# Last stage of a vision tower kernel: paired decay banks, one scan over two groups, sums with h on TensorE and ScalarE, three of 24 C products on VectorE

## What is computed

```python
t = _unfold3(t, 2).transpose(0, 2, 1)
h = t @ proj_w.T + proj_b
# layer 0: h = h + ssm(layernorm(h)); h = h + ffn(layernorm(h))
A_bar = jnp.exp(dA)                                   # dA = delta * A
B_bar = (A_bar - A) / dA * delta[..., None] * Bproj[:, :, None, :]
def step(h, inp):
    a, b, c, xl = inp
    h = a * h + b * xl[..., None]
    y = jnp.einsum('bn,bdn->bd', c, h)
    return (h, y)
# ffn: a router picks one of 8 experts of 64 columns for each token (argmax), gelu, times its probability
```

## Time and profile before

| | |
|---|---|
| median of 3 runs | 9341.66 us (9338.44 to 9353.73) |
| profiled execution, device time | 9346.65 us |
| its span, first to last instruction | 9344.9 us |
| mean granted TensorE clock | 0.890 of full speed |
| last stage | from about 3640 us to the end |
| busy, share of the span | PE 82%, DVE 67%, ACT 45%, POOL 68% |

### The profile page before, as it was taken

How to read it: one execution, slowest core, us unless ns; L and a number is a source line. 1 busy time by engine, 2 the same in 40 slices (tenths; PEclk the granted TensorE clock), 3 DMA queues, 4 the chain that set the end, 5 groups by cost and what they waited for, 6 DMA issues and landing times.

```text
span 9344.9 us, 86112 instructions
## 1 busy us (share of the span) xinstructions
PE 7616.6 (82%) x30892; PEld 3189.1 (34%) x30892; DVE 6306.6 (67%) x8010; ACT 4247.4 (45%) x6801; POOL 6400.6 (68%) x2483
## 2 busy tenths in 40 slices
PE   6799999777999985578788778788778788777777
PEld 3444444223444432223333323333323333323333
DVE  1355555441233344888888888888888888888885
ACT  1366666553344432444444444444444444444442
POOL 0011111116766614999999999999999999999995
PEclk9999999998999987788888888888888888888887
DMA  0011111115444413223322323322323322323321
GB/s 25 25 39 43 44 42 38 31 31 105 96 102 97 101 37 99 84 95 115 108 97 91 118 90 119 108 97 89 118 90 118 110 97 89 116 93 112 110 97 51
DMA packets 356851, 786.54 MB, mean 84 GB/s; under 512 B 70437, under 2 KB 282806, under 8 KB 348936
## 3 DMA queue, kind: packets, MB, share of 16 engines
q1 hardware_dynamic: 320376, 690.75, 24.6%
q0 software_dynamic: 21712, 51.75, 2.2%
q10 hardware_dynamic: 14336, 38.54, 1.2%
HBM read 597.36 MB, written 183.35 MB: 84 GB/s over the span
## 4 chain that ended last, share of the span: by engine, by line
PE 25%; DVE 16%; POOL 9%; issue 8%; ACT 4%; DMA 0%; SPq 0%; DVEq 0%; POOLq 0%
PE ps L1492 7%; DVE v L1793 7%; DVE v L1802 7%; PE ps L1499 5%; PE ps L1497 5%; POOL v L1460 5%; POOL v L1450 4%; PE ps L1535 2%; PE ps L1488 2%; PE ps L1595 2%; DVE dl L1784 1%; ACT ps L1691 1%; ACT gm L1716 1%; ACT dl L1668 0%; DVE gm L1870 0%
## 5 line engine op out<-in xcount | busy, mean ns | idle before, releaser
L1691 ACT ACTIVATE ps<-dr,aa 128x448 f32<-128x448 f32 x2688 | 1695.8, 635 | 2649.4 <-DVE v L1802 2631.3
L1450 POOL TENSOR_TENSOR v<-xr,bt 128x1792 f32<-128x1792 f32 x672 | 2683.0, 3993 | 203.2 <-PE ps L1535 105.5
L1460 POOL TENSOR_TENSOR v<-v,ct 128x1792 f32<-128x1792 f32 x672 | 2690.2, 4003 | 177.7 <-ACT st L1681 177.1
L1802 DVE TENSOR_TENSOR_SCAN v<-ps,st,v 128x448 f32<-128x448 f32 x2304 | 2629.1, 1141 | 0.0
L1793 DVE SCALAR_TENSOR_TENSOR v<-ps,aa,v 128x448 f32<-128x448 f32 x2688 | 1786.6, 665 | 660.5 <-POOL v L1450 357.5
L222 POOL DMA_DIRECT2D tokens<-ob x448 | 235.4, 532 | 1883.4 <-ACT ob L383 1833.3
L1595 PE MATMUL ps<-w_or_w,gm 128*112 128x384 f32 x1792 | 737.2, 562 | 453.6 <-DVE gm L1870 382.2
L1535 PE MATMUL ps<-v,dg 128*32 128x448 f32 x5376 | 719.6, 610 | 218.5 <-POOL v L1460 217.9
L1595 PEld LDWEIGHTS ps<-w_or_w,gm 128*112 128x112 f32 x1792 | 340.5, 200 | 867.9 <-DVE gm L1870 424.6
L1492 PE MATMUL ps<-h,w_or_w 128*128 128x448 f32 x1344 | 538.4, 551 | 14.1 <-DVE gm L1837 14.1
L1488 PE MATMUL ps<-sq,jm 128*128 128x448 f32 x672 | 344.7, 658 | 191.2 <-ACT ot L1725 183.3
(11 more groups left out here) (318 smaller groups left out, 11777.1 us busy)
## 6 DMA issues: line engine op xcount, KB each, us to landing
xr<-h_by_channel SPq DMA_DIRECT2D x168, 896.0 KB, 4.7
dr<-delta_by_channel SPq DMA_DIRECT2D x168, 896.0 KB, 5.6
x<-tokens SPq DMA_DIRECT2D x252, 224.0 KB, 5.2
tokens<-ob POOLq DMA_DIRECT2D x448, 112.0 KB, 2.4
w_or_w<-in_w SPq DMA_DIRECT2D x29, 1536.0 KB, 6.3
w_or_w<-centred_w SPq DMA_DIRECT2D x27, 1536.0 KB, 6.4
h_by_channel<-h SPq DMA_DIRECT2D x112, 336.0 KB, 10.8
delta_by_channel<-dl SPq DMA_DIRECT2D x112, 336.0 KB, 5.1
```

Source lines behind the costliest of these rows:

```text
L1450: tt(v[:, n % RING], xr[:, dc % 2], bt[:, q:q + 1, :].to_broadcast([128, 4, T]), ALU.mult).then_inc(s_v, 1)
L1460: tt(v[:, n % RING], v[:, n % RING], ct[:, q:q + 1, :].to_broadcast([128, 4, T]), ALU.mult).then_inc(s_cm, 1)
L1691: fn(bank((4 * n + g) % 3), dr[:, dc % 2, g, :], ACT.Exp, scale=aa[:, 4 * k + g:4 * k + g + 1]).then_inc(s_a, 1)
L1802: nc.vector.tensor_tensor_scan(v[:, n % RING, g, :], bank((4 * n + g) % 3), v[:, n % RING, g, :], 0.0 if first else st[:, 4 * k + g:4 * k ...
```

## The change

Only `tail` changes.

- **Decays in two pairs of banks.** PSUM banks 0 to 3 hold the decays of a step's four groups: groups 0 and 1 side by side in banks 0 and 1 (the second starts at column 450 and crosses into the next bank), groups 2 and 3 in banks 2 and 3. The column ahead of each group is zero and stays so. A pair is written anew when the scan of that pair of the step before is done.
- **One scan over two groups.** v gets 449 columns for each group. ScalarE (`start_states`) writes the kept states into column 0 of the four groups ahead of its decays; the zero decay there restarts the recurrence. VectorE's order is now weigh, weigh, scan of the pair, weigh, weigh, scan of the pair; each scan waits for the weigh just ahead of it.
- **Three own steps**, k = 5, 13 and 21: VectorE scans each group alone, in place in the decay bank, and multiplies the pair with C itself. GpSimd leaves out `weigh_out` there. ScalarE copies the last states from the decay bank (`free_pair`) before it writes new decays over them.
- **h plus sums by TensorE and ScalarE.** TensorE adds h to the sum by a product with the identity as last of each chunk; ScalarE copies the result into h (`add_to_h`). In ScalarE's queue it stands ahead of the decays of step 4 dc + 7, and of step 3 for the last chunk.
- **One bank of sums** (bank 4) where there were two. TensorE starts a chunk when ScalarE has copied the chunk before.
- **RING = 6** where it was 5. To find room, ms, sel32, ai, encb and wm live in other tiles, and the means of every third unit in bcs.

```diff
-RING = 5
-YB, BS, BX, BF = 3, 5, 6, 7
+RING = 6
+AR, YB, BS, BX, BF = 4, 4, 5, 6, 7
+OWN = (5, 13, 21)
+def others(n):
+    i, k = divmod(n, STEPS)
+    return i * (STEPS - len(OWN)) + sum(j not in OWN for j in range(k + 1))
+def owned(n):
+    return n + 1 - others(n)
...
+        def decay(g):
+            at = g // 2 * 1024 + g % 2 * (T + 1)
+            return flat[:, at + 1:at + T + 1]
...
-        v = sb("v3", [128, RING, 4, T])
+        v = sb("v3", [128, RING, 4, T + 1])
...
@@ GpSimd, weigh_out @@
+                if k in OWN:
+                    return
...
@@ TensorE, step @@
                 if q == 0:
-                    after(pe, s_hy, DC * i + dc - 1)
-                pe.wait_ge(s_cm, n + 1)
+                    after(pe, s_hy, DC * i + dc)
+                if k in OWN:
+                    pe.wait_ge(s_cv, 2 * owned(n))
+                else:
+                    pe.wait_ge(s_cm, others(n))
...
+                if q == Q - 1:
+                    mm(bank(YB), ident[:, :], h[:, i % 3, dc, :], start=False, stop=True).then_inc(s_hs, 1)
...
@@ ScalarE @@
+            def start_states(i, k):
+                n = STEPS * i + k
+                if k in OWN:
+                    return
+                after(act, s_ns, n + 1 - RING)
+                if i >= 1:
+                    act.wait_ge(s_st, others(n - STEPS))
+                fn(v[:, n % RING, :, 0], st[:, 4 * k:4 * k + 4], ACT.Copy,
+                   scale=0.0 if i % J3 == 0 else 1.0).then_inc(s_s0, 1)
+            def free_pair(n, pair):
+                i, k = divmod(n, STEPS)
+                if k in OWN:
+                    act.wait_ge(s_cv, 2 * owned(n) + pair - 1)
+                    at = 4 * k + 2 * pair
+                    fn(st[:, at:at + 2], decays(pair)[:, :, T - 1], ACT.Copy).then_inc(s_sv, 1)
+                    act.wait_ge(s_sv, 2 * owned(n) + pair - 1)
+                else:
+                    act.wait_ge(s_sc, 2 * others(n) + pair - 1)
+            def add_to_h(i, dc):
+                act.wait_ge(s_hs, DC * i + dc + 1)
+                if dc == 0:
+                    act.wait_ge(s_xst, 64 * (i + 1))
+                fn(h[:, i % 3, dc, :], bank(YB), ACT.Copy).then_inc(s_hy, 1)
...
                 for g in range(4):
-                    after(act, s_sc, 4 * n + g - 2)
-                    fn(bank((4 * n + g) % 3), dr[:, dc % 2, g, :], ACT.Exp,
+                    if g % 2 == 0 and n > 0:
+                        free_pair(n - 1, g // 2)
+                    fn(decay(g), dr[:, dc % 2, g, :], ACT.Exp,
                        scale=aa[:, 4 * k + g:4 * k + g + 1]).then_inc(s_a, 1)
...
+                    if i >= 1 and k == 3:
+                        add_to_h(i - 1, DC - 1)
+                    if i < UNITS and k >= 7 and k % 4 == 3:
+                        add_to_h(i, k // 4 - 1)
                     if i < UNITS:
+                        start_states(i, k)
                         step(i, k)
...
@@ VectorE @@
+            def scan(i, k, pair):
+                n = STEPS * i + k
+                row = v[:, n % RING, 2 * pair:2 * pair + 2, :].rearrange("p g t -> p (g t)")
+                if pair == 0:
+                    dve.wait_ge(s_s0, others(n))
+                dve.wait_ge(s_wt, 4 * n + 2 * pair + 2)
+                nc.vector.tensor_tensor_scan(row, flat[:, 1024 * pair:1024 * pair + 2 * T + 2], row, 0.0, ALU.mult,
+                                             ALU.add).then_inc(s_sc, 1)
+            def own_scan(i, k, pair):
...
+                for g in range(2 * pair, 2 * pair + 2):
+                    dve.wait_ge(s_wt, 4 * n + g + 1)
+                    nc.vector.tensor_tensor_scan(decay(g), decay(g), v[:, n % RING, g, 1:T + 1],
+                                                 0.0 if first else st[:, 4 * k + g:4 * k + g + 1], ALU.mult,
+                                                 ALU.add).then_inc(s_sp, 1)
...
+                tt(v[:, n % RING, 2 * pair:2 * pair + 2, 1:T + 1], decays(pair),
+                   ct[:, k % Q:k % Q + 1, :].to_broadcast([128, 2, T]), ALU.mult).then_inc(s_cv, 1)
             def step(i, k):
-                for g in range(4):
-                    weigh(i, k, g)
-                    if g > 0:
-                        scan(i, k, g - 1)
...
+                for pair in range(2):
+                    weigh(i, k, 2 * pair)
+                    weigh(i, k, 2 * pair + 1)
+                    if k in OWN:
+                        own_scan(i, k, pair)
+                    else:
+                        scan(i, k, pair)
-            def add_to_h(i, dc):
...
+            nc.vector.memset(ps[:, 0:AR, :], 0.0).then_inc(s_set, 1)
```

More of the change, by code:

```diff
@@ L1174, in bank, with decays @@
             return ps[rows, k, 0:n]
+        flat = ps[:, :, :].rearrange("p k n -> p (k n)")
+        def decay(g):
+            at = g // 2 * 1024 + g % 2 * (T + 1)
+            return flat[:, at + 1:at + T + 1]
+        def decays(pair):
+            row = flat[:, 1024 * pair:1024 * pair + 2 * T + 2]
+            return row.rearrange("p (g t) -> p g t", g=2)[:, :, 1:T + 1]
         ident = sb("ident3", [128, 128])
         jm = sb("jm768", [128, 128])
-        sel32 = sb("sel32", [128, 32])
         desc = sb("desc", [CH, NCH, NX])
@@ L1314, in tail, with means @@
         ROUTE, TAIL = 9, 28
+        def means(i):
+            return mu[few, i % 3, :] if i % 3 < 2 else bcs[few, :]
         def pair_bank(o):
@@ L1384, in spread_c @@
                 if i < UNITS:
-                    after(sp, s_cm, STEPS * (i - 1) + STEPS - Q + q + 1)
+                    for own in (True, False):
+                        k = max((k for k in range(q, STEPS, Q) if (k in OWN) == own), default=None)
+                        if i >= 1 and k is not None:
+                            n = STEPS * (i - 1) + k
+                            sp.wait_ge(s_cv if own else s_cm, 2 * owned(n) if own else others(n))
                     spread_row(ct[:, q, :], i, 1, q).then_inc(s_lc[q], 16)
@@ L1702, in mlp @@
                     act.wait_ge(s_mean, i + 1)
-                    fn(ms[:, :], bank(BX), ACT.Square).then_inc(s_ms, 1)
+                    fn(rs2[:, :], bank(BX), ACT.Square).then_inc(s_ms, 1)
                 if k == A_RS2:
@@ L1791, in weigh @@
                     dve.wait_ge(s_v, n + 1)
-                dve.wait_ge(s_a, 4 * n + g + 1)
-                stt(v[:, n % RING, g, :], bank((4 * n + g) % 3), aa[:, 4 * k + g:4 * k + g + 1], v[:, n % RING, g, :],
-                    ALU.subtract, ALU.mult).then_inc(s_wt, 1)
-            def scan(i, k, g):
+                dve.wait_ge(s_a, 4 * n + g // 2 * 2 + 2)
+                row = v[:, n % RING, g, 1:T + 1]
+                stt(row, decay(g), aa[:, 4 * k + g:4 * k + g + 1], row, ALU.subtract, ALU.mult).then_inc(s_wt, 1)
@@ L1797, in scan @@
                 n = STEPS * i + k
                 first = i % J3 == 0
-                if g == 0 and not first:
-                    dve.wait_ge(s_st, n + 1 - STEPS)
-                dve.wait_ge(s_wt, 4 * n + g + 1)
-                nc.vector.tensor_tensor_scan(v[:, n % RING, g, :], bank((4 * n + g) % 3), v[:, n % RING, g, :],
-                                             0.0 if first else st[:, 4 * k + g:4 * k + g + 1], ALU.mult,
-                                             ALU.add).then_inc(s_sc, 1)
@@ L1806, in step @@
-            def step(i, k):
-                for g in range(4):
-                    weigh(i, k, g)
-                    if g > 0:
-                        scan(i, k, g - 1)
-                    elif k > 0:
-                        scan(i, k - 1, 3)
-                    elif i > 0:
-                        scan(i - 1, STEPS - 1, 3)
-            def add_to_h(i, dc):
-                dve.wait_ge(s_ns, STEPS * i + Q * (dc + 1))
-                if dc == 0:
-                    dve.wait_ge(s_xst, 64 * (i + 1))
-                tt(h[:, i % 3, dc, :], h[:, i % 3, dc, :], bank(YB + dc % 2), ALU.add).then_inc(s_hy, 1)
+                if not first:
+                    dve.wait_ge(s_sv, 2 * owned(n - STEPS) + pair - 1)
@@ new lines, in own_scan @@
+                for g in range(2 * pair, 2 * pair + 2):
[3 more added lines that the diff above has]
+                                                 ALU.add).then_inc(s_sp, 1)
+                if k // Q == 0 and pair == 0:
+                    dve.wait_ge(s_lc[k % Q], 16 * (i + 1))
@@ L1825, in mlp @@
                     dve.wait_ge(s_var[1], DC * (i + 1))
-                    tt(bank(BS), bank(BS), ms[:, :], ALU.subtract).then_inc(s_vr, 1)
+                    tt(bank(BS), bank(BS), rs2[:, :], ALU.subtract).then_inc(s_vr, 1)
                 if k == V_ENC:
@@ L1863, in mlp @@
                     after(dve, s_o, 2 * NCH * i)
[L1864 removed]
+                    tt(oh8, ps[few, BX, 0:T], means(i), ALU.add).then_inc(s_oh, 1)
                 for m in range(MT):
@@ L1909, in _ @@
                         step(i, k)
-                    elif k == 0:
-                        scan(UNITS - 1, STEPS - 1, 3)
```

(4 more changed lines are left out.)

40 lines of the change are left out of this document (23 added, 17 removed).

## The result

The changed kernel takes 9245.88 us (median of four runs, 9242.9 to 9254.01) where the kernel before, on the same chip, takes 9346.51: a ratio of 0.9894 (95% interval 0.9877 to 0.9911). The profiled execution took 9242.9 us, its span is 9241.1 us and its mean TensorE clock 0.913 of full speed (before: 9346.65, 9344.9 and 0.890). The forecast was 9290, a gain of some 52 us; the gain is 100. The direction and the place are as forecast, the size is about twice.

A forecast was written before the change was run, and what follows sets the result against it. Bound: a circle of VectorE, ScalarE-TensorE hand-overs, then TensorE alone. 1.8 x 26 units = 47, plus about 10 for unit 0, less 3 and 2 at the ends: 9346.65 - 52 = 9295, 9290 against the median; range 9195 to 9370.

The forecast's parts named there:

- The circle: One unit runs VectorE, then ScalarE-TensorE hand-overs, then TensorE alone; GpSimd last only between steps 23 and 3; 201.3 us becomes 199.5.
- the third stretch: From the squares to the means, TensorE without a gap: 73.7 us as before plus 1.6 for two products with h.
- outputs 4 to 7: TensorE's outputs with sums behind step 23: three at about 5.3 us, one at 7.7, h 0.78, done at T + 118.6.
- The first units: Unit 0, paced by GpSimd alone: three products fewer come through in full, about 10 us saved.
- The ends: Start longer by about 2 us (between 0 and 4) for clearing four banks, end longer by 3 for waits for TensorE.
- The scan: VectorE's joined scan over 898 columns takes 1.93 us to its successor; a pair 3.22 instead of 3.27, a step 6.43.
- (c): Rival: VectorE's joined scan saves nothing, costing 2.10 us or more; a unit takes 202.2, the kernel about 9365; chance 0.13.
- The dependent scan: VectorE, 16 pairs: if chained semaphores cost nothing extra, 0.11 us each, some 1.8 a unit, about 9243; forecast went by the row.
- (a): Rival: GpSimd's three products come through in full, 11.8 us a unit, 9028 or 9025 against the median; chance 0.05.
- (b): Rival: ScalarE isn't held by TensorE in step 23; some 6 us a unit less, about 9130; chance 0.12.
- (d): Rival: whole kernel shows no change that can be told, the same terms with errors that cancel; chance 0.20.
- nobody waiting for GpSimd with six buffers: With 6 buffers GpSimd's waits for a sum (60.8 us in 15 units) go, but nobody waits for GpSimd then.

The follow-up runs named there:

- e2: Changed kernel with output product 3 moved from TensorE's step 18 to step 19, behind the sum and the product with h: 9093.88 us, ratio to before 0.9733.
- e3: Changed kernel with ScalarE's copy of h put behind the decays of its step instead of ahead of them: 9113.16 us, ratio to before 0.9758.
- e7: Changed kernel without the product of h with the identity, so h is left out of the sums: 9135.99 us, ratio to before 0.9767.
- e6: Kernel before with only the layout of v changed, 449 columns a group, data in columns 1 to 448: 9288.48 us, ratio to before 0.9932.
- e1: Changed kernel with no own steps, GpSimd multiplying all 24 steps with C again: 9097.99 us, ratio to before 0.9729.
- e8: Changed kernel with each joined scan over 898 columns cut into two over 449: 9164.13 us, ratio to before 0.9802.
- e11: One own step, k = 5, added to the 8948.16 us kernel (no own steps, output 3 late, addition behind decays, two scans): 8955.2 us.
- e4: Changed kernel with 5 buffers of v instead of 6 (RING = 5): 9258.62 us, ratio to before 0.9909.

## Why the prediction was right in direction and half in size

**The circle is right.** All marks of the unit laid out in the prediction can be held against the rows: B row T + 24.6, read T + 24.6, gap 0.8, read 0.48; output 3 T + 82.7, read T + 82.9; step 23 T + 92.4 with a wait of some 5 us, read T + 92.8 and 5.24; output 4 T + 94.2, read T + 94.4; squares T + 122.2, read T + 121.6; ScalarE's waits for h 8 and 3, read 8.12 and 2.59. e2 and e3 show that this hold is the cause, not only beside it. GpSimd at 872 of 1000 is near the 890 named, and TensorE is without a gap for its stretch.

**The term that was mis-sized: the third stretch.** I laid 75.3 us from the squares to the means, 73.7 as before plus two products with h. It takes 6084.73 - 6010.49 = 74.2. The 73.7 came from a unit in which the squares stood behind a wait of 6.77 us and took 4.85; behind 1.84 us they take 4.09 (granted clock 0.50 and 0.61 in these stretches). I carried the price of a slow start over, though my own change shortened the wait in front of it. In the 25 intervals of before this wait is 6.7 to 7.5 us and the squares take 4.8 each time; in those of after it is 1.84 each time and they never take more than 4.2. That is 0.8 of the 1.1 us. The other 0.3 is at least in part the two products with h, which I laid at 1.6: without them (e7) C is 1.3 us shorter where the squares take 2.52 in both kernels, and 1.5 where they take about 4.2. With 0.6 from outputs 4 to 7 it makes 1.7, where a mean unit gained 3.3 us instead of the 1.8 laid: over 25 units some 38 us.

**The first units: 20.8 us instead of 10.** I priced the three products there and missed that the layout makes every `weigh_out` 0.32 us shorter. e6, which has the layout alone, shows 9.1 there; e1, which has no own steps, takes 316.5 for the two intervals where after takes 308.1, so the own steps are worth 8.4. My 10 was for these. The remaining 3.3 are in other parts of the change, and I didn't take them apart.

**The ends.** The start was laid at +2 and stands at +5.3, inside the scatter of 27 us of that mark. Behind the last mark I laid +3; it is -5.7. One and a half units run there, and they gain their 3.3 each as well, which I had not counted. I didn't take it further apart.

**The scan: nearly right, by two errors.** The scan to its successor is 1.94 to 1.95, laid 1.93. But the start behind the weighs is 1.28 to 1.37, where I had 0.59 + 0.70 = 1.29: the first pair of a step has 0.08 more. A step is 6.55, not 6.43, so against 6.54 before nothing is saved: the premise of rival (c) holds on VectorE, but not its price of 2.7 us a unit, since the successor of the scan comes at 1.95 and not at 2.10. Eight steps of 0.12 more are 1.0 us, yet output 3 starts only 0.2 later than laid: 0.3 came back at the B row, and the rest lies in terms of mine that were too high and that I didn't take apart. Against the kernel before the step is the same, and that made it no slower.

**The dependent scan.** By the Trainium skill, "VectorE: DVE Perf Modes", "The DRAIN you can't avoid", a semaphore between chained instructions costs nothing extra, and the prediction gave 9243 for that. The time is 9246, yet the rule isn't what brought it. The Trainium skill has it from eight copies; here the rows of after and e8 show the scan that waits for the weigh just ahead starting 1.28 to 1.37 us after the pair of weighs, and the scan that waits for the weigh one further back 1.17 to 1.19 after it. That is 0.1 to 0.2 us, so on this chain the trace doesn't agree.

**The other rivals.** (a), GpSimd's products in full, 9025: excluded by e1 and e11. (b), ScalarE not held at step 23, 9130: not what the change does, but e2 and e3, which bring it about, take 9094 and 9113, so its price was about right. (d), no change, is outside the interval. Two of the times were added up a little off: less the same 5 as the forecast, (a) comes to 9023 and (c) to 9360. And nobody waiting for GpSimd with six buffers is right (after has no wait of VectorE for it), but e4 shows that with five VectorE would wait: part of what the circle gained rests on the sixth buffer.

## What to carry to other kernels

Before an engine is relieved, follow one period of the loop and ask in each stretch who is last; relief pays only there, and only if the engine that takes the work over doesn't feed the relieved one. When a wait is moved ahead of an instruction that others need (here the addition ahead of the decays), price what is queued behind it: this order alone cost 133 us, more than the whole change gained. When a change shortens a wait, don't carry over durations from behind the old wait. And compare kernels stretch by stretch: e4 lost 2.2 us in one stretch and got about as much back from faster products in others, so the whole time alone said that the buffer was worth next to nothing.
